# Cross attention with a gate: probabilities turned once in fp32, split behind the turn, loads in another order

## The reference

```python
qp = q @ Wq + bq
kp = k @ Wk + bk
vp = v @ Wv + bv
w = softmax(einsum('bqd,bkd->bqk', qp, kp) / sqrt(512))
x = einsum('bqk,bkd->bqd', w, vp)
gate = concatenate((qp, x), axis=-1) @ Wg + bg
out = x * mask[..., None] * sigmoid(gate) + q
```

## Time and profile before

| | us |
|---|---|
| median of 3 runs | 432.78 (431.98 to 433.77) |
| the profiled execution | 434.12 |
| its span, first to last instruction | 432.3 |
| PE busy | 417.7 (97%) |
| DVE, ACT, POOL busy | 215.5, 151.9, 126.8 |
| mean granted clock of PE | 0.992 |

### The profile page before, as it was taken

One profiled execution on the slowest core, in us unless ns is written; L12 is line 12 of the kernel. 1 busy time (PEld: TensorE's weight loads), 2 busy tenths in 40 slices (PEclk: granted clock), 3 DMA queues, 4 the chain that ended last, 5 costly groups with the idle time before them and its releaser, 6 DMA issues.

```text
span 432.3 us, 5334 instructions
## 1 busy us (share of the span) xinstructions
PE 417.7 (97%) x1940; PEld 335.3 (78%) x1940; DVE 215.5 (50%) x385; ACT 151.9 (35%) x283; POOL 126.8 (29%) x98
## 2 busy tenths in 40 slices
PE   8999999998996999999999999999999999999996
PEld 4879978886774787787877878787787878778784
DVE  4786546553450646354463634546253553725453
ACT  5644243224222243241423324143342424324131
POOL 0004154346524051340505225050432505143100
PEclk9999999999898999999999999999999999999999
DMA  8975434457589766957577595766758567685312
GB/s 271 389 276 213 143 83 192 155 205 226 195 243 265 249 182 228 291 158 259 187 229 237 182 278 167 240 199 231 226 198 277 162 230 211 216 253 194 119 49 97
DMA packets 43125, 90.86 MB, mean 210 GB/s; under 512 B 5276, under 2 KB 5276, under 8 KB 42460
## 3 DMA queue, kind: packets, MB, share of 16 engines
q1 hardware_dynamic: 42524, 89.48, 63.5%
q10 hardware_dynamic: 576, 1.05, 0.6%
HBM read 63.51 MB, written 27.00 MB: 209 GB/s over the span
## 4 chain that ended last, share of the span: by engine, by line
PE 90%; DMA 5%; DVE 2%; ACT 1%; POOL 1%; SPq 1%; issue 0%; DVEq 0%; ACTq 0%
PE bank L414 40%; PE bank L322 31%; PE bank L437 4%; PE bank L438 4%; PE bank L444 3%; PE bank L445 3%; DMA v_ext<-v_dram 2%; PE bank L424 2%; PE bank L427 2%; DMA x_raw<-in_xT 1%; DMA wqT_raw<-in_wqT 1%; PE bank L383 1%; PE bank L365 1%; DMA v_dram<-v_st 1%; POOL v_st L731 1%
## 5 line engine op out<-in xcount | busy, mean ns | idle before, releaser
L414 PE MATMUL bank<-wqg,xT 128*128 128x512 f32 x768 | 191.8, 396 | 0.0
L414 PEld LDWEIGHTS bank<-wqg,xT 128*128 128x128 f32 x768 | 142.8, 189 | 29.4
L731 POOL TENSOR_TENSOR xT<-x_raw,xT 128x512 fp32r<-128x512 f32 x64 | 87.9, 1403 | 191.3 <-ACT xT L478 191.3
L695 DVE SCALAR_TENSOR_TENSOR prod_sb<-tanh_sb,bank 128x512 f32<-128x512 f32 x64 | 43.9, 686 | 123.1 <-ACT tanh_sb L550 123.1
L550 ACT ACTIVATE tanh_sb<-bank 128x512 f32<-128x512 f32 x64 | 38.4, 599 | 129.3 <-PE bank L438 121.7
L706 DVE SCALAR_TENSOR_TENSOR out_sb<-prod_sb,half_mask,x_rows 128x512 f32<-128x512 f32 x64 | 49.1, 768 | 1.7
L322 PE MATMUL bank<-xT,mt 128*77 128x512 f32 x192 | 47.1, 394 | 0.0
L322 PEld LDWEIGHTS bank<-xT,mt 128*77 128x77 f32 x192 | 28.0, 146 | 15.7
L478 ACT ACTIVATE xT<-x_raw 128x512 fp32r<-128x512 f32 x64 | 35.2, 617 | 3.2 <-DMA x_raw<-in_xT 3.2
L322 PE MATMUL bank<-wg,vT 128*128 128x512 f32 (+1 forms) x120 | 30.7, 407 | 2.6 <-DVE vT L577 2.6
L322 PE MATMUL bank<-wv,ctxT 128*128 128x512 f32 (+1 forms) x120 | 30.2, 401 | 0.0
(11 more groups left out here) (75 smaller groups left out, 378.7 us busy)
## 6 DMA issues: line engine op xcount, KB each, us to landing
x_raw<-in_xT SPq DMA_DIRECT2D x64, 256.0 KB, 5.2
x_rows<-in_x SPq DMA_DIRECT2D x64, 256.0 KB, 3.7
out_y<-out_sb SPq DMA_DIRECT2D x64, 256.0 KB, 2.0
v_ext<-v_dram SPq DMA_DIRECT2D x32, 308.0 KB
v_dram<-v_st SPq DMA_DIRECT2D x18, 512.0 KB, 3.2
v_ext<-v_dram SPq DMA_DIRECT2D x16, 180.0 KB
ctxT_raw<-in_ctxT SPq DMA_DIRECT2D x4, 624.0 KB, 10.7
ctx_rows<-in_ctx SPq DMA_DIRECT2D x4, 616.0 KB
```

Of the source, the lines that this page charges most:

```text
L414: pe.matmul(gate_ps[n % 3][:, :], xT[b % 2][:, s, c, q], wqg[:, m, c, :], start=(c == 0 and (s, m) == PRODUCTS[0]), stop=False)
L695: dve.scalar_tensor_tensor(prod_sb[:, n % 2, :], tanh_sb[:, n % 2, :], 1.0, attn_ps[n % 2][:, :], ALU.add, ALU.mult).then_inc(prod_made, 1)
L731: pool.tensor_tensor(dst, src, f32(hi_), ALU.subtract).then_inc(made, 1)
```

## The change

- The probabilities stay in fp32 and are written once with 96 columns a tile: the 77 keys, and again the last 19 of them (`prob`, two multiplications on DVE). The split ahead of the transposes and `stack_probs` are gone.
- PE turns them with 4 transposes a batch in place of 8, and does so after 15 matmuls of the batch in place of 18; 9 gate matmuls follow ahead of `attend(b, 0)` in place of 6.
- Behind the transposes ACT makes the high part from the bank (96 rows of `wT`), and from that, within SBUF, two copies of 32 rows (`high_probs`). DVE makes the low part from the bank (`low_probs`). Rows 77 to 95 of the second half of `wT` are zeroed once.
- `v_ext` is loaded by five DMAs in place of four, to fit the new rows.
- SP loads x transposed and by rows of batch 0 one step of the value loop earlier, and at the loop's end `v_ext` of batch 0 ahead of x transposed of batch 1.

```diff
-LO_A = 45
-LO_B = S - LO_A
-K_A, K_B = S + LO_A, S + LO_B
+
+
+Q = 32
+TOP = 3 * Q
+DUP = S - (TOP - S)
+K_B = TOP + DUP - Q
...
-        w_a = sb("w_a", D0 + 6272, [P, T, K_A])
-        w_b = sb("w_b", D0 + 6784, [P, T, K_B])
+        prob = sb("prob", D0 + 6272, [P, T, TOP])
...
-                sync.dma_start(f32(v_ext[i][S:K_A, 0, :]), v_dram[r:r + LO_A, LO, :]).then_inc(vext_in[i], 16)
-                sync.dma_start(f32(v_ext[i][S:K_B, 1, :]), v_dram[r + LO_A:r + S, LO, :]).then_inc(vext_in[i], 16)
+                sync.dma_start(f32(v_ext[i][S:TOP, 0, :]), v_dram[r + DUP:r + S, LO, :]).then_inc(vext_in[i], 16)
+                sync.dma_start(f32(v_ext[i][TOP:P, 0, :]), v_dram[r:r + Q, LO, :]).then_inc(vext_in[i], 16)
+                sync.dma_start(f32(v_ext[i][S:K_B, 1, :]), v_dram[r + DUP - (K_B - S):r + DUP, LO, :]).then_inc(vext_in[i], 16)
...
-                if k == 5:
+                if k == 4:
                     sync.wait_ge(dots_made, DOT["sb", 3] + 1)
                     load_xT(0, (0, 1))
+                if k == 5:
+                    load_xT(0, (2, 3))
                 if k == 6:
-                    load_xT(0, (2, 3))
-                if k == 7:
                     sync.wait_ge(dots_made, DOT["sb", 7] + 1)
                     load_rows(0, 0)
                     load_rows(0, 1)
-                if k == 8:
+                if k == 7:
                     load_rows(0, 2)
                     load_rows(0, 3)
-            sync.wait_ge(xT_lo, C)
-            load_xT(1)
             sync.wait_ge(job_done, J["v", KT - 1] + 1)
             wait_stored(2)
             load_vext(0)
+            sync.wait_ge(xT_lo, C)
+            load_xT(1)
             load_vext(1)
...
                 if b == 0:
                     pe.wait_ge(job_drained, last_in_bank(6))
                 else:
-                    pe.wait_ge(wTb_made, b)
+                    pe.wait_ge(shift_made, b)
...
             def turn_probs(b):
-                pe.wait_ge(prob_split, b + 1)
-                pe.wait_ge(stacked_a, b + 1)
-                pe.wait_ge(stacked_b, b + 1)
+                pe.wait_ge(prob_made, b + 1)
+                pe.wait_ge(prob_twice, b + 1)
                 if b == 0:
                     pe.wait_ge(job_drained, last_in_bank(7))
+                else:
+                    pe.wait_ge(wTb_made, b)
+                    pe.wait_ge(wT_lo, b)
                 for t in range(T):
-                    last = pe.transpose(turn_ps[0:K_A, t * P:(t + 1) * P], w_a[:, t, :], ident[:, :])
-                last.then_inc(wa_turned, 1)
-                for t in range(T):
-                    last = pe.transpose(score_ps[0:K_B, t * P:(t + 1) * P], w_b[:, t, :], ident[:, :])
-                last.then_inc(wb_turned, 1)
+                    last = pe.transpose(turn_ps[0:TOP, t * P:(t + 1) * P], prob[:, t, :], ident[:, :])
+                last.then_inc(turned, 1)
...
                     pe.wait_ge(wTa_made, b + 1)
                     pe.wait_ge(wTb_made, b + 1)
-                    pe.wait_ge(vext_in[b % 2], 64 * (b // 2 + 1))
+                    pe.wait_ge(wT_lo, b + 1)
+                    pe.wait_ge(vext_in[b % 2], 80 * (b // 2 + 1))
                 ps = gate_ps[n % 3]
-                pe.matmul(ps[:, :], wT[0:K_A, 0, q], v[0:K_A, 0, D:2 * D], start=False, stop=False)
+                pe.matmul(ps[:, :], wT[:, 0, q], v[:, 0, D:2 * D], start=False, stop=False)
                 pe.matmul(ps[:, :], wT[0:K_B, 1, q], v[0:K_B, 1, D:2 * D], start=False, stop=True).then_inc(gate_done, 1)
...
             turn_scores(0)
             for b in range(B):
                 more = b + 1 < B
                 gate_main(b, 0)
-                gate_main(b, 1, range(0, C // 2))
+                gate_main(b, 1, range(0, 1))
                 turn_probs(b)
-                gate_main(b, 1, range(C // 2, C))
+                gate_main(b, 1, range(1, C))
                 attend(b, 0)
...
-            def stack_probs(b):
-                act.wait_ge(prob_hi, b + 1)
-                act.activation(w_a[:, :, S:K_A], w_a[:, :, 0:LO_A], ACT.Copy).then_inc(stacked_a, 1)
-                act.activation(w_b[:, :, S:K_B], w_a[:, :, LO_A:S], ACT.Copy).then_inc(stacked_b, 1)
+            def high_probs(b):
+                act.wait_ge(turned, b + 1)
+                if b == 0:
+                    act.wait_ge(wT_zeroed, 1)
+                else:
+                    act.wait_ge(attn_done, b * T)
+                act.activation(wT[0:TOP, 0, :], turn_ps[0:TOP, :], ACT.Copy).then_inc(wT_top, 1)
+                act.wait_ge(wT_top, b + 1)
+                act.activation(wT[TOP:P, 0, :], wT[0:Q, 0, :], ACT.Copy).then_inc(wTa_made, 1)
+                act.activation(wT[TOP:P, 1, :], wT[Q:2 * Q, 0, :], ACT.Copy).then_inc(wTb_made, 1)
...
             exps(0)
             for b in range(B):
                 more = b + 1 < B
-                stack_probs(b)
+                high_probs(b)
                 if more:
                     xT_hi_of(b + 1)
-                act.wait_ge(wa_turned, b + 1)
-                act.activation(wT[0:K_A, 0, :], turn_ps[0:K_A, :], ACT.Copy).then_inc(wTa_made, 1)
-                act.wait_ge(wb_turned, b + 1)
-                act.activation(wT[0:K_B, 1, :], score_ps[0:K_B, :], ACT.Copy).then_inc(wTb_made, 1)
                 tanh_tile(b, 0)
                 tanh_tile(b, 1)
                 tanh_tile(b, 2)
...
-                dve.tensor_tensor(prob[:, :, :], expd[:, :, :], rinv[:, :].unsqueeze(2).broadcast_to([P, T, S]), ALU.mult).then_inc(prob_made, 1)
-                dve.wait_ge(prob_made, b + 1)
-                dve.tensor_copy(w_a[:, :, 0:S].bitcast(F32R), prob[:, :, :]).then_inc(prob_hi, 1)
-                dve.wait_ge(prob_hi, b + 1)
-                dve.tensor_tensor(w_b[:, :, 0:S].bitcast(F32R), prob[:, :, :], w_a[:, :, 0:S], ALU.subtract).then_inc(prob_split, 1)
+                if b:
+                    dve.wait_ge(turned, b)
+                dve.tensor_tensor(prob[:, :, 0:S], expd[:, :, :], rinv[:, :].unsqueeze(2).broadcast_to([P, T, S]), ALU.mult).then_inc(prob_made, 1)
+                dve.tensor_tensor(prob[:, :, S:TOP], expd[:, :, DUP:S], rinv[:, :].unsqueeze(2).broadcast_to([P, T, TOP - S]), ALU.mult).then_inc(prob_twice, 1)
+
+            def low_probs(b):
+                dve.wait_ge(wT_top, b + 1)
+                dve.tensor_tensor(wT[0:S, 1, :], turn_ps[0:S, :], f32(wT[0:S, 0, :]), ALU.subtract).then_inc(wT_lo, 1)
...
+            dve.wait_ge(job_done, J["v", KT - 1] + 1)
+            dve.memset(f32(wT[2 * Q:TOP, 1, :]), 0.0).then_inc(wT_zeroed, 1)
             softmax_max(0)
             softmax_rest(0)
+            dve.wait_ge(wT_zeroed, 1)
             for b in range(B):
                 more = b + 1 < B
+                low_probs(b)
                 product(b, 0)
```

More of the change, by code:

```diff
@@ L145, in build @@
         rinv = sb("rinv", H0 + 3424, [P, T])
-        prob = shifted
         qk_in = [sem(f"qk_in{c}") for c in range(C)]
@@ L173, in build @@
         sum_made, rinv_made, prob_made = sem("sum_made"), sem("rinv_made"), sem("prob_made")
-        prob_hi, prob_split = sem("prob_hi"), sem("prob_split")
-        stacked_a, stacked_b = sem("stacked_a"), sem("stacked_b")
-        wa_turned, wb_turned, wTa_made, wTb_made = sem("wa_turned"), sem("wb_turned"), sem("wTa_made"), sem("wTb_made")
+        prob_twice, turned = sem("prob_twice"), sem("turned")
+        wT_zeroed, wT_top, wTa_made, wTb_made, wT_lo = sem("wT_zeroed"), sem("wT_top"), sem("wTa_made"), sem("wTb_made"), sem("wT_lo")
         gate_done, attn_done = sem("gate_done"), sem("attn_done")
@@ L443, in attend @@
                 ps = attn_ps[n % 2]
-                pe.matmul(ps[:, :], wT[0:K_A, 0, q], v[0:K_A, 0, 0:D], start=True, stop=False)
+                pe.matmul(ps[:, :], wT[:, 0, q], v[:, 0, 0:D], start=True, stop=False)
                 pe.matmul(ps[:, :], wT[0:K_B, 1, q], v[0:K_B, 1, 0:D], start=False, stop=True).then_inc(attn_done, 1)
```

## The result

The kernel after takes 453.16 us (median of 4 runs, 452.53 to 453.67) beside 433.27 (431.98 to 434.62) for the kernel before, measured beside it: a ratio of 1.0458, 95% interval 1.0421 to 1.0495. It is 4.6% slower. The prediction was 444, range 435 to 455. The direction was as forecast and the time lies inside the range, but the time is 9 us longer than forecast, and two terms of the sum fared very differently.

The account below looks back on a forecast made before the run. The prediction took PE to bound the kernel, with 3.00 us of slack for POOL's x chunks; 19.5 (loop) - 8.0 (loads) - 0.2 (batch 15) = +11.3 us on the profiled execution, giving a median of 444, range 435 to 455.

Parts of the forecast that it names:

- The loop's term: Loop over batches: POOL's later start delays the scores by 1.39 us a batch, 14 x 1.39 = 19.5 us.
- The slack holds: Rival for the loop: POOL's start moves by less than 2.6 us, every part pays, 419 us; chance 0.07.
- Its steps: ACT's chain in a batch: transposes, bank copy, two 32-row copies, x; POOL starts at 6.48, ends 12.06, scores at 12.37.
- POOL and DVE met as forecast: POOL's window in a batch: one DVE output inside, four chunks stay 5.58 us; when both meet, the later waits.
- POOL meets no output: Rival for POOL's window in a batch: loss of 0.8 us a batch, total 436 or 434 us; chance 0.08.
- The clock rival: PE's clock falls behind the idle in the loop: 467 us if every batch, 455 if every second; chance 0.13.
- The loads' term: Value loop's end and batch 0: earlier loads bring the third tile's attention 8.0 us forward; bounds 4.3 and 10.1.
- with the same bytes to move: Step for batch 0's first tanh: the last store still lands 17.9 us behind that point of SP's queue, at 136.3.
- The loads bring only the first wait: Rival for batch 0's loads: DMAs are full and `v_ext` lands no sooner, 448 us; chance 0.08.
- batch 15: Last batch, which has no scores: -0.35 for fewer transposes and +0.13 at `attend(b, 0)`, -0.2 us.
- The saved transposes: PE in each batch: four fewer worth 0.35 us, 5.6 in 16 batches, but vanishing in the wait for the scores.

Follow-up runs that it names:

- E1: Kernel after, with ACT making the four high chunks of the next batch's x ahead of the probabilities' copies from batch 1 on: 431.89 us, ratio 0.9921.
- E3: Kernel after, with the 19-row load of `v_ext` cut into 16 and 3 rows, one DMA more: 447.14 us, ratio 1.0276.
- E6: Kernel before, with its 45-row load of `v_ext` cut into 19 and 26 rows, nothing else: 439.96 us, ratio 1.0128.
- E7: Kernel after, with the 19-row load of `v_ext` cut into 17 and 2 rows: 452.57 us, ratio 1.0434.
- E4: Kernel after, with x's chunks ahead of the copies from batch 1 on and the 19 rows cut into 16 and 3: 425.52 us, ratio 0.9777.
- E8: Kernel before, with the new order of loads alone and its own four `v_ext` DMAs: 431.35 us, ratio 0.9912.
- E9: E4 with the transposes after 12 gate matmuls, 12 behind them in place of 9: 422.97 us, ratio 0.9735.
- E2: Kernel after, with one more 32-row copy a batch on ACT into a spare tile, ahead of the two there: 460.6 us, ratio 1.0584.

## Why the prediction was right in one half and wrong in the other

- **The loop's term was right.** Forecast: 1.39 us a batch, a period of 20.1, scores at 12.37, idle of about 1.5. Measured: 1.30 in the mean of 14 batches, and in batch 4 a period of 20.01, scores at 12.23, idle of 1.27. E1 shows the cause to be the one named: ACT's copies ahead of x moved POOL by more than the 3.00 us of slack. *The slack holds* fell with it.
- **Its steps were off and cancelled, which was luck.** The 32-row copies are 0.65 apart, not 0.52 as x's 128-row chunks: the upper bound of that step, and POOL starts at 6.70 in place of 6.48. On the other side POOL took 5.47 in place of 5.58, and the scores follow its end within 0.06, where I had put 0.31: the 0.23 from weight load to first matmul in the earlier trace rows isn't paid here, where weight load and matmul wait for the same tile.
- **POOL and DVE met as forecast.** One output in POOL's window took 1.61, another ran its 0.75 or little more (0.84 for the next tile); the mean of L712 rose from 768 (L706 before) to 961 ns. *POOL meets no output* fell. One row of the prediction was read too sharply: the output of 152.47 that waited is stamped 0.05 ahead of its POOL chunk (152.52), so that row doesn't show that the later one waits. The output at 220.05 does: it began while POOL's second and third chunk ran (218.59 to 221.12), took 1.61 and so ended behind them, and the fourth chunk (from 221.08) took 1.72.
- **The clock did not fall.** With some 1.3 us of idle in nearly every batch the mean granted clock is 0.996, beside 0.992 before. The clock rival, the dearest, fell. It did fall behind the single wait of 3.29 us: the stretch 132 to 136 has 0.65, and in E3, without that wait, it has 1.00.
- **The loads' term was wrong:** -8.0 forecast, +0.2 measured at the start of batch 1. The step that failed is "with the same bytes to move": I took the time from SP's issue to the last store's landing as fixed by bytes and queue order. The bytes were nearly the same, but the 19-row pieces are 152 KB that by the 6.4% share, the packets and E3, E6 and E7 went through one engine, and the last store landed (143.6) some 4 us after the other engines had run dry (139.7). The 19-row DMA was in the diff; I priced it as an issue of 0.4 us on SP's queue and looked at no further cost. *The loads bring only the first wait* was the nearest rival (448), but for another reason: while ACT waited for the last store, the DMAs were not full, they were nearly idle.
- **Inside the range by its width.** 453.16 lies in 435 to 455, but not because the sum was right. For the profiled execution it gave 445.4, and 452.87 was measured. Of these 7.5, read from the timelines to a few tenths: 8.2 too little for the loads, 1.3 too much for the loop, 0.4 too little for batch 15. (Another 1.6 between 444 and 453.16 is where the profiled executions lay in their groups.) The range reached that far up for a falling clock, which did not come; no rival named what did.
- **With that mended** (E3) the loads bring the third tile forward from 145.89 to 139.44, 6.45 us, and the total is 447.1: within the bounds of the term (4.3 to 10.1), 1.5 short of the 8.0. The first tanh then stands at 138.07, not 136.3. Of these 1.8 us 1.1 were there before the first `v_ext` load: SP issued it at 119.53 (119.63 in the kernel after), where I had put 118.4; 0.92 of the wait ahead of it on PE had stayed. The rest is the way from there to the store's landing, 18.5 in place of 17.9.
- **The saved transposes** were worth nothing while PE waited, as forecast. E4 and E8 differ by 5.8 us; the four transposes were put at 5.6 in all. That the two numbers meet is no proof, since the loads of these kernels differ too: E4's batch 1 begins at 144.83, E8's at 147.57, and that is half of it. The periods tell more: 18.50 in E1 is 0.22 less than the 18.72 of before, 18.33 in E9 is 0.39 less, where 0.35 was forecast.

## What to carry to other kernels

Before moving work onto an engine, write down what stands behind it in that engine's queue and how much slack each of those has; E1 shows that the same instructions cost 21 us more or less by their place alone. Price a DMA not by its bytes only but by how its rows divide: a piece with an awkward number of rows can hold up every later transfer that shares its engine, and the sign of it is a wait for a DMA while the DMAs' share is near a sixteenth. Where PE waits twice in a batch for the same chain, the idle in front of the last wait doesn't measure what the chain costs (E2).

## What the runs showed of the hardware that was not expected

- A DMA of 19 or of 17 rows held a store back by 5 to 6 us, while one of 16 rows and one of 3 didn't (E3, E7). During the tail 23 to 29 GB/s moved.
- On ACT a copy of 32 rows within SBUF took 0.63 us, as long as one of 128 rows (620 ns), and successive ones started 0.54 to 0.66 apart (E2 and the timeline of after), against 0.53 for x's four chunks (2.20 less 0.62, by three). What decides between 0.54 and 0.65 wasn't tried.
